# Adding the expert outputs of layer 0: GpSimd's six blocks shared out to TensorE, ScalarE and VectorE

## The reference, cut to what matters

```python
xn = _layernorm(x, axis=-1)
x = x + _L0_attn_ref(xn, ...) + _L0_ffn_ref(xn, ...)
xn = _layernorm(x, axis=-1)
x = x + _L1_attn_ref(xn, ...) + _L1_ffn_ref(xn, ...)
```

## Time and profile before

| what | us |
|---|---|
| median of three runs | 1195.58 |
| the profiled execution | 1195.94 |
| its span, first to last instruction | 1194.1 |
| VectorE busy | 947.3 |
| GpSimd busy | 783.2 |
| ScalarE busy | 545.1 |

### The profile page before, as it was taken

How to read it: one execution, slowest core, us unless ns; L and a number is a source line. 1 busy time by engine, 2 the same in 40 slices (tenths; PEclk the granted TensorE clock), 3 DMA queues, 4 the chain that set the end, 5 groups by cost and what they waited for, 6 DMA issues and landing times. The chain is left out here.

```text
span 1194.1 us, 21002 instructions
## 1 busy us (share of the span) xinstructions
PE 1015.1 (85%) x7025; PEld 881.0 (74%) x7025; DVE 947.3 (79%) x1636; ACT 545.1 (46%) x1511; POOL 783.2 (66%) x685
## 2 busy tenths in 40 slices
PE   5636777799999999999844699999779999999994
PEld 4612333368888887888733699999679999999994
DVE  7887999999999999999999874112358777778848
ACT  1301111157888787888714583000045555555541
POOL 3147766648888888888879357777625656655530
PEclk9868877899999999999956889999979999999998
DMA  9923233325665565656363032999612222442239
GB/s 284 367 104 134 103 116 125 118 69 158 177 183 176 170 175 157 192 175 170 104 279 126 37 103 83 382 366 387 233 48 66 70 66 70 138 141 64 64 112 347
DMA packets 119884, 192.20 MB, mean 161 GB/s; under 512 B 16426, under 2 KB 88190, under 8 KB 117730
## 3 DMA queue, kind: packets, MB, share of 16 engines
q1 hardware_dynamic: 100896, 154.30, 40.4%
q0 software_dynamic: 17408, 35.32, 8.1%
q10 hardware_dynamic: 1474, 1.24, 0.4%
HBM read 123.77 MB, written 67.03 MB: 160 GB/s over the span
## 5 line engine op out<-in xcount | busy, mean ns | idle before, releaser
L557 POOL DMA_INDIRECT y_tok<-FF,yidx x278 | 299.7, 1078 | 171.4 <-DVE FF L1436 110.0
L549 POOL DMA_INDIRECT sorted_x<-XN,idx x256 | 248.5, 971 | 95.5 <-issue 82.3
L884 PEld LDWEIGHTS ps<-FF 128*128 128x128 f32 x1680 | 196.2, 192 | 12.0 <-issue 9.0
L884 PE MATMUL ps<-FF 128*128 128x128 f32 x1680 | 205.0, 275 | 0.0
L346 POOL TENSOR_TENSOR BG<-TPB 128x2048 f32<-128x2048 f32 (+1 forms) x42 | 160.9, 3860 | 14.3 <-DVE BG L1265 13.9
L1274 DVE TENSOR_TENSOR BG<-ps,TPB 128x1024 f32<-128x1024 f32 x128 | 147.3, 1212 | 0.0
L915 PE MATMUL ps<-BG,cst 128*128 128x512 f32 x176 | 106.0, 770 | 47.9 <-DVE BG L1239 47.9
L1283 DVE TENSOR_REDUCE BG<-BG 128x256 f32<-128x4096 f32 x32 | 139.5, 4358 | 0.0
L866 PE MATMUL ps<-FF 128*128 128x256 f32 x568 | 134.5, 380 | 0.0
L915 PEld LDWEIGHTS ps<-BG,cst 128*128 128x128 f32 x176 | 43.0, 251 | 105.7 <-issue 54.7
L628 ACT ACTIVATE FF<-ps,FF 128x256 f32<-128x256 f32 x284 | 115.1, 480 | 7.4 <-PE ps L866 7.1
(11 more groups left out here) (229 smaller groups left out, 2048.3 us busy)
## 6 DMA issues: line engine op xcount, KB each, us to landing
FF<-in_moe SPq DMA_DIRECT2D x71, 514.0 KB
sorted_x<-TPB SPq DMA_DIRECT2D x36, 520.0 KB, 4.4
FF<-in_kpad SPq DMA_DIRECT2D x18, 1024.0 KB, 10.6
FF<-sorted_x SPq DMA_DIRECT2D x135, 130.0 KB, 2.2
TPB<-in_kpad SPq DMA_DIRECT2D x14, 1024.0 KB, 11.1
BG<-y_tok SPq DMA_DIRECT2D x12, 1024.0 KB, 9.6
y_tok<-FF,yidx POOLq DMA_INDIRECT x278
xt_d<-BG SPq DMA_DIRECT2D x16, 256.0 KB, 4.3
```

Of the source, the lines that this page charges most:

```text
L549: pool.indirect_dma_start(sorted_x[layer], bass.IndirectOffsetOnAxis(ap=idx[:, k, j:j + 1], axis=0), XN[:, j, :], None).then_inc(s_sc[part ...
L557: pool.indirect_dma_start(y_d[layer], bass.IndirectOffsetOnAxis(ap=yidx[:, G % 4, r:r + 1], axis=0), ys[:, G % 4, r * D:(r + 1) * D], None ...
L884: t = pe.matmul(psY[:, r * P:(r + 1) * P], hT[:, G % 2, m, r * P:(r + 1) * P], (wc[:, G % 4, :] if layer == 0 else block_weights(f, r))[:, ...
```

## The change

GpSimd keeps blocks 0 and 1. Blocks 2 to 5 are added on TensorE in halves of four rows (`add_outputs`): X, y2 and y1 are multiplied by the identity, one after another, into one PSUM bank (512 columns), and ScalarE copies the bank back into `X` (`store_added`). Halves 0 to 3 (blocks 2, 3) stand in the loop over steps, after the transposes of heads 29 and 30; halves 4 to 7 (blocks 4, 5) stand between the transposes and gates of groups 1 to 3. VectorE adds blocks 6 and 7 at the start of quarter 2 instead of quarter 3. The root of quarter 0 moves before the copies of halves 2 and 3, and the root of quarter 1 to behind the first copy of a group and the copy of half 4. `s_comb` counts four blocks for layer 0 instead of eight. The core of the diff:

```diff
-ADD_POOL = 6
+ADD_POOL = 2
+ADD_PE = (2, 3, 4, 5)
+COMBINED = 8 - len(ADD_PE)
 COUNTS_AT = 5
...
         s_comb = sem("combined")
+        s_addps = sem("block_halves_added_psum")
+        s_addx = sem("block_halves_added")
         s_resst = sem("x1_stored")
...
+        def add_bank(n):
+            return (psH[0], psH[1], psH[2], psT)[n] if n < 4 else (psY, psT)[n % 2]
         def heads_bank(b):
...
                 sp.wait_ge(s_oev, 2 * i + 2)
-                sp.wait_ge(s_comb, 8 + i + 1)
+                sp.wait_ge(s_comb, COMBINED + i + 1)
                 k, b0 = i // 4, (i % 4) * 8
...
                         sp.wait_ge(s_wd, NF1)
-                    wait(sp, s_comb, 8 + i - 3 if layer == 1 and i >= 4 else 0)
+                    wait(sp, s_comb, COMBINED + i - 3 if layer == 1 and i >= 4 else 0)
                     sp.dma_start(outputs(layer, i).rearrange("p c n -> p (c n)"),
...
             for i in range(8):
-                sp.wait_ge(s_comb, i + 1)
+                if i in ADD_PE:
+                    sp.wait_ge(s_addx, 2 * ADD_PE.index(i) + 2)
+                else:
+                    sp.wait_ge(s_comb, i + 1 if i < ADD_POOL else i + 1 - len(ADD_PE))
                 sp.dma_start(res_d[:, i * 1024:(i + 1) * 1024], X2[:, i * 1024:(i + 1) * 1024]).then_inc(s_resst, 16)
...
                     .then_inc(s_xup, 1)
+            def store_added(n):
+                act.wait_ge(s_addps, n + 1)
+                j = 8 * ADD_PE[n // 2] + 4 * (n % 2)
+                act.copy(X[:, j:j + 4, :].rearrange("p a d -> p (a d)"), add_bank(n)[:, :]).then_inc(s_addx, 1)
...
                         pair_heads(b - 3)
+                    if c == max(len(tiles), 3) - 1 and NPAIR <= b < NPAIR + 2:
+                        if b == NPAIR + 1:
+                            std_dev(5, 0, 16, 2)
+                        for n in range(2):
+                            store_added(2 * (b - NPAIR) + n)
...
-            std_dev(5, 0, 16, 2)
             for q in range(4):
...
                     copy_xT(1, g)
-                if q < 3:
+                    if q == 0:
+                        store_added(4 + g)
+                        if g == 0:
+                            std_dev(6, 16, 32, 2)
+                if q == 0:
+                    store_added(7)
+                elif q < 3:
                     std_dev(6 + q, 16 * q + 16, 16 * q + 32, 2)
...
             act.activation(lg, lg, ACT.Exp).then_inc(s_ex, 1)
-            act.wait_ge(s_comb, 8)
+            act.wait_ge(s_comb, COMBINED)
             for u in range(NT // 2):
...
+            def add_outputs(n):
+                i, h = ADD_PE[n // 2], n % 2
+                if n == 0:
+                    pe.wait_ge(s_gelu, NF)
+                    pe.wait_ge(s_xsT, NF)
+                if h == 0:
+                    pe.wait_ge(s_yl[i], 16)
+                    pe.wait_ge(s_xup, 4 * i + 4)
+                wait(pe, s_addx, n - 1 if n > 4 else 0)
+                out = add_bank(n)[:, :].rearrange("p (k d) -> p k d", k=4)
+                y = outputs(0, i)[:, 4 * h:4 * h + 4, :]
+                pe.matmul(out, ident, X[:, 8 * i + 4 * h:8 * i + 4 * h + 4, :], start=True, stop=False)
+                pe.matmul(out, ident, y[:, :, D:2 * D], start=False, stop=False)
+                pe.matmul(out, ident, y[:, :, 0:D], start=False, stop=True).then_inc(s_addps, 1)
             def transposes_and_gates(layer, wg):
                 if layer == 1:
+                    pe.wait_ge(s_addx, 4)
                     pe.wait_ge(s_xup, NPAIR)
...
                         gates(g - 1)
+                    if layer == 1 and 1 <= g <= 3:
+                        add_outputs(3 + g)
+                        if g == 3:
+                            add_outputs(7)
                 gates(NG - 1)
...
                         heads_T(b - 3)
+                    if c == max(len(tiles), 3) - 1 and NPAIR <= b < NPAIR + 2:
+                        for n in range(2):
+                            add_outputs(2 * (b - NPAIR) + n)
...
                 dve.tensor_tensor(dv, dv, y[:, :, 0:D], ALU.add).then_inc(s_comb, 1)
-                dve.wait_ge(s_comb, 8 * layer + i + 1)
+                dve.wait_ge(s_comb, COMBINED + i + 1 if layer else i + 1 - len(ADD_PE))
...
             for q in range(4):
-                dve.wait_ge(s_xup, 8 * q + 8)
+                if q == 2:
+                    dve.wait_ge(s_xup, NPAIR)
+                    for i in (6, 7):
+                        combine(0, X, i)
+                elif q < 2:
+                    dve.wait_ge(s_xup, 8 * q + 8)
                 for i in (2 * q, 2 * q + 1):
-                    if i < ADD_POOL:
+                    if i in ADD_PE:
+                        dve.wait_ge(s_addx, 2 * ADD_PE.index(i) + 2)
+                    elif i < ADD_POOL:
                         dve.wait_ge(s_comb, i + 1)
-                    else:
-                        combine(0, X, i)
                 stats_of(X, 16 * q, 16 * q + 16)
...
                 inverse_root(5 + q, 16 * q, 16 * q + 16, 2).then_inc(s_shift, 1)
```

## The result

The changed kernel takes 1203.95 us (median of four runs, 1202.75 to 1205.8) beside 1195.24 for the kernel before (1194.91 to 1197.18): a ratio of 1.0069, 95% interval 1.0056 to 1.0083, so **8.7 us slower** where 1200.0 was forecast. Run again later (E7) it was 1.0046 (1.0029 to 1.0063). The profiled execution took 1203.31 us, 7.37 more than the one of before; its span is 1201.5.

The account below looks back on a forecast made before the run. VectorE's row numbers, hence when `choose` begins, were taken to bound the kernel: 2.9 us late plus 1.5 for clock falls, 4.4 on 1195.94 gives 1200.3; medians run 0.36 lower, so 1200.0 us, own range 1198 to 1203, widened to 1195 to 1204.5.

Parts of the forecast that it names:

- Sign and mechanism: Slower: VectorE gains 12.3 us, but TensorE's products and ScalarE's copies delay heads, roots and gates; `choose` 4.4 us late.
- The gain: In quarter 0, VectorE gets back 12.3 us lost in seven instructions stretched during GpSimd's additions.
- Steps 1 to 3: Last heads and quarter 0: first half-block at 616.6 after block 2's load, shift at 630.2, `attention_added` complete at 635.8.
- Step 4: Normalised rows, copy 0, gates 0, half 4, its copy, root of quarter 1 at 644.0; VectorE waits some 7 us; shift 645.4.
- Step 5: Copies 1 and 2, gates 1 and 2, halves 5 to 7: 12.3 us, to 656.3; statistics and variance of quarter 2 at 660.9.
- step 6: ScalarE's copy 3, eight rows, copies 4 to 6 with gates between; root 662.7, shift of quarter 2 about 664.2.
- Step 7: Quarter 3, without additions: shift at 673.0, then 3.4 us to `choose` at 676.4, 2.9 us late.
- one fall costs half a block's difference, about 3 us: TensorE's clock falling to half after a pause before gates; 1.5 us added as the middle between none and one.
- Everything after `choose` moves by the same 4.4 us: From `choose` to the end: the 4.4 us delay carries through unchanged, with TensorE's 12.4 us of spare time kept.
- Faster: Quarters 1 and 2: VectorE runs without waits and keeps its 12.3 us; `choose` near 661, kernel 1183.3 us; chance 0.08.
- Same: Through quarter 2's statistics: TensorE at full clock from its first half; `choose` at 673.4, kernel 1195.5 us; chance 0.17.
- Much slower: TensorE stays at half clock, eight halves at 5.1 us, gates and transposes doubled; 34 us late, 1230 us; chance 0.05.

Follow-up runs that it names:

- E1: The kernel before, with GpSimd's additions of blocks 2 to 5 left out and nothing in their place; 1183.93 us, ratio 0.9889.
- E9: The changed kernel with halves 4 to 7 left out, so no engine adds blocks 4 and 5; root of quarter 1 behind the first copy; 1191.39 us.
- E4: The changed kernel plus idle TensorE products: four before the wait for block 2, two before the first transposes, one before gates 0; 1201.7 us, ratio 1.0035.
- E10: The changed kernel plus idle TensorE products: nine before the wait for block 2, two before the first transposes, one before gates 0; 1201.05 us, ratio 1.0036.
- E2: The changed kernel with the root of quarter 1 put before the copy of half 4 instead of behind it; 1201.0 us, ratio 1.0032.
- E5: The kernel before with 48 idle products of 8 columns (96 instructions) on TensorE behind the second half of the convolution; 1198.29 us, ratio 1.0015.
- E6: The changed kernel with 80 idle products of 8 columns (160 instructions) on TensorE behind the convolutions; 1198.61 us, ratio 1.0013.
- E3: The changed kernel with blocks 4 and 5 moved from TensorE to VectorE; root of quarter 1 behind the first copy; 1195.78 us, ratio 0.9990.

## Why the prediction was right, and where it was short

**Sign and mechanism: right.** The gain was named and sized (12.3 us; E1 shows it, with 10.3 reaching `choose`), and so was what takes it back: halves in the same in-order streams as heads, gates and roots (E9). In E1's trace `by_sums` takes 0.43 us for 2.27, and the other six of the seven stretched instructions 0.17 to 0.19 for 1.42 to 2.32. In the kernel before each of the seven ended 0.03 to 0.27 us after one of GpSimd's additions did; the statistics at 623.74 were not stretched beside the same additions (3.18 us, as at 642.70). Why some are held and others not, no run shows.

**Steps 1 to 3** hold to about 1 us: half 0 began at 616.70 (616.6 predicted), the shift of quarter 0 was done at 629.15 (630.2), the last copy of heads near 635 (635.8).

**Step 4** had the wait of VectorE (9.63 us, some 7 predicted) in its place, but counted gates 0 and half 4 at 3.5 us. They took 6.3, because the clock had fallen in TensorE's pause ahead of them (E4 and E10, which fill that pause, have 3.6): 0.55 granted from 638.58 to 644.90. The shift of quarter 1 was thus done at 647.17 for 645.4.

**Step 5** carried this on (the last half copied at 658.2 for 656.3), and **step 6** added the second fall: gates of quarter 2 in the window at 0.57, the shift at 667.32 for 664.2. **Step 7** arrives 3.3 us past its 676.4.

**The term that was mis-sized is the clock**: "one fall costs half a block's difference, about 3 us", taken at 1.5 us as the middle between none and one. Both pauses that the prediction named were followed by half clock. Gates 0 and half 4 took 2.8 us longer than their 3.5. From the first transposes of quarter 2 to the third gates it was 4.8 us (660.25 to 665.05), where quarter 1 of the kernel before took 3.4 at full clock (650.70 to 654.14), so the second fall cost some 1.4 us, an estimate from these rows. Half 0 was 0.7 us cheaper than its 5.1. By these figures 2.9 + 2.8 + 1.4 - 0.7 gives 6.4 us, beside 6.2 measured.

**"Everything after `choose` moves by the same 4.4 us" failed as well**: a 0.8 us wait of VectorE for the route totals went in this execution (E7's has it again; the clock granted in the 4.5 to 4.8 us ahead of it was 0.82 here, 0.53 before and 0.64 in E7), and the last stage grew by 2.4. Predicted 1200.3 for the profiled execution, measured 1203.31: 1.8 of the difference lie ahead of `choose`, the rest behind it.

**The number fell inside the range partly by luck.** The forecast's own range was 1198 to 1203, and the median of 1203.95 lies above it, inside only the 1204.5 that had been kept for part of a stretch at half clock. By the prediction's own 3 us for a fall, two falls give 1198.5 + 6 = 1204.5 and not 1203. The delay was 8.7 us where 4.4 were forecast, 5.5 in E7.

**The rivals.** *Faster*: its test was the last half copied by 644; it came at 658.2. *Same*: its mechanism, full clock from the first half, was made in E10, whose time stays above that of the kernel before (1.0023 to 1.0048). *Much slower*: the clock did rise with half 0 (0.59 granted from 616.70 to 621.15, 1.00 from there to 637). The lengths of a half, 2.6 and 5.1 us by the rows of 256 columns, held: its three fp32 products of 512 columns took 2.6 us at full clock, and 5.25 at half clock (E7, 616.36 to 621.61, 0.50 granted).

## What to carry to other kernels

Before work is handed to an engine with time to spare, find the stretch in which it is idle in the order of its own stream: the same halves cost 9.7 us in front of the gates that the chain waits for, and those of one block made nobody wait after them. If TensorE pauses and then carries the chain, price its first work at both clocks: here half clock followed the pauses ahead of gates 0 and of quarter 2 (0.50 granted from 638.5 to 643, 0.57 from 661 to 665), and in the kernel before full clock followed one of 3.4 us (below). The longest wait of a list names who came last, not what to move: E2 took a 9.63 us wait away and gained nothing on this path.

## What was not expected

- **The clock differs between executions of the same code.** In E5 nothing is changed ahead of `choose`, and its profiled execution had `choose` 53.9 us behind `by_sums`, 1.9 later than in the kernel before. The windows from 666.5 to 675 show 0.70 granted in E5 (first line) and 0.98 in the kernel before (second line):

```profile
666.50:675.00 8.50, 5.28 (x31) 5.09 (x31) 5.25 (x25) 5.25 (x14) 2.77 (x7) 0.70 0.03 11
666.50:675.00 8.50, 4.12 (x32) 3.50 (x30) 5.88 (x24) 5.57 (x15) 1.96 (x5) 0.98 0.00 1
```

TensorE's timelines, E5 and then the kernel before, show the same transposes after nearly the same pause, at half clock and at full clock:

```profile
672.65 1.11 PE L832 MATMUL ps<-cst,xg 128*128 128x128 f32 x4 [3.22 <-ACT xg L721]
...
671.84 0.66 PE L832 MATMUL ps<-cst,xg 128*128 128x128 f32 x4 [3.42 <-ACT xg L721]
```

In E6's twelve executions the four fastest (up to 1197.06 us) have a mean granted clock of 0.939 to 0.941, the four slowest (from 1200.29 us on) 0.934 to 0.936; which of the two follows from the other is not shown. Differences of 1 to 2 us between single profiled executions decide nothing here; those of E1, E3 and E9 to the changed kernel are well above that.

- **A store and a load of unchanged size got longer** at the end of the kernel (4.9 for 3.6 us, 12.2 for 9.7) with nothing in that stage changed. By E5 and E6 the place of TensorE's code accounts for part of it at most; the cause stays open.
